# Graph attention kernel, edge loop: three PSUM buffers for the edge products, the softmax in one bank with its key rows read from DRAM, and a later place for sums and exponents

## What is computed

```python
q, k, v = x @ Wq + bq, x @ Wk + bk, x @ Wv + bv      # by head
e  = edge_attr @ We                                  # 106250 x 256 by 256 x 256
kj = k[src] + e
alpha = sum(q[dst] * kj, over the 32 of a head) / sqrt(32)
amax  = segment_max(alpha, dst)
ea    = exp(alpha - amax[dst])
denom = segment_sum(ea, dst)
out   = segment_sum((v[src] + e) * ea / denom[dst], dst) + (x @ Ws + bs)
```

## Time and profile before

| | us |
|---|---|
| median of 3 runs | 2530.81 |
| lowest and highest | 2526.67, 2532.15 |
| the profiled execution, its time | 2519.88 |
| its span in the profile | 2518.1 |
| first and last addition L1059 of the edge loop | 230.1, 1905.4 |
| busy share of the span: PE, DVE, ACT, POOL | 94%, 79%, 62%, 72% |

### The profile page before, as it was taken

The page is one execution under the profiler, slowest core; times in us unless marked ns, Lnnn a source line. Parts: engine busy times, 40 slices in busy tenths (PEclk is TensorE's granted clock), DMA queues, the critical chain, the costliest instruction groups (busy, mean ns, idle before and its releaser), DMA issues. The chain is left out here.

```text
span 2518.1 us, 62222 instructions
## 1 busy us (share of the span) xinstructions
PE 2368.8 (94%) x13314; PEld 1994.0 (79%) x13315; DVE 1990.4 (79%) x5253; ACT 1573.8 (62%) x4349; POOL 1809.0 (72%) x2137
## 2 busy tenths in 40 slices
PE   6998999999999999999999999999995658999998
PEld 2445888888888888888888888888883647999998
DVE  6875999999999999999999999999997872222222
ACT  1122677777777777777777777777774125666665
POOL 4223788888888888888888888888886205666666
PEclk9999999999999999999999999999998558999999
DMA  7325877788788778778877777777772672433443
GB/s 230 129 107 182 243 230 229 227 233 232 225 232 228 222 231 232 230 230 232 233 230 229 232 223 231 233 226 227 232 229 81 193 224 53 71 63 63 69 67 54
DMA packets 337730, 476.37 MB, mean 189 GB/s; under 512 B 61382, under 2 KB 268556, under 8 KB 337116
## 3 DMA queue, kind: packets, MB, share of 16 engines
q0 software_dynamic: 92576, 259.72, 39.2%
q1 hardware_dynamic: 238556, 213.23, 27.7%
q10 hardware_dynamic: 6288, 0.05, 0.2%
HBM read 425.40 MB, written 50.57 MB: 189 GB/s over the span
## 5 line engine op out<-in xcount | busy, mean ns | idle before, releaser
L818 POOL DMA_INDIRECT kv_ring<-vk_table,tab_c x880 | 859.7, 977 | 250.9 <-issue 168.2
L976 PE MATMUL ps_e<-we_sb,aT 128*128 128x256 f32 x3520 | 916.4, 383 | 12.3 <-DVE ve_ke L1065 7.8
L976 PEld LDWEIGHTS ps_e<-we_sb,aT 128*128 128x128 f32 x3520 | 600.6, 191 | 82.7 <-issue 31.3
L1059 DVE TENSOR_TENSOR ve_ke<-kv_ring,ps_e 128x512 f32<-128x512 f32 x880 | 601.4, 683 | 47.9 <-PE ps_e L980 17.9
L828 POOL TENSOR_TENSOR ve_ke<-ve_ke 128x256 f32<-128x256 f32 x880 | 551.2, 630 | 16.9 <-ACT factor L945 3.3
L1029 PE MATMUL ps_u<-ve_ke,sel 128*128 128x264 f32 x1760 | 544.3, 391 | 10.1 <-DVE node_slots L1135 5.6
L980 PE MATMUL ps_e<-q_slots,selT 128*128 x1760 | 517.2, 375 | 0.0
L905 ACT COPY aT<-ps_t 128x256 f32<-128x256 f32 x880 | 325.4, 370 | 283.6 <-PE ps_t L960 246.9
L1135 DVE TENSOR_TENSOR node_slots<-node_slots,ps_u 128x264 f32 x880 | 369.9, 420 | 29.0 <-PE ps_u L1029 25.0
L980 PEld LDWEIGHTS ps_e<-q_slots,selT 128*128 128x128 f32 x1760 | 334.7, 190 | 45.6
L1047 DVE TENSOR_REDUCE alpha<-ve_ke 128x8 f32<-128x256 f32 x880 | 362.9, 412 | 2.0
(11 more groups left out here) (255 smaller groups left out, 2631.3 us busy)
## 6 DMA issues: line engine op xcount, KB each, us to landing
a_ring<-in_edge_attr SPq DMA_DIRECT2D x880, 128.0 KB
loc_c<-loc_table SPq DMA_DIRECT2D x220, 128.0 KB, 3.9
kv_ring<-vk_table,tab_c POOLq DMA_INDIRECT x880
vk_table<-kv_out SPq DMA_DIRECT2D x49, 256.0 KB, 2.0
skip_table<-skip_out SPq DMA_DIRECT2D x49, 128.0 KB, 1.7
skip<-skip_table SPq DMA_DIRECT2D x7, 896.0 KB, 9.5
xn_table<-node_slots SPq DMA_DIRECT2D x7, 896.0 KB, 5.1
w_sb<-in_L_ffn_W SPq DMA_DIRECT2D x2, 2048.0 KB, 10.1
```

The lines of the kernel that those rows point to most:

```text
L818: g.indirect_dma_start(out=kv_ring[:, i % N_KV, :], out_offset=None, in_=vk_table, in_offset=bass.IndirectOffsetOnAxis(ap=tab_c[:, c % N_T ...
L976: t.matmul(ps_e[i % 2][:, 0:D], aT[i % 2][:, k * P:(k + 1) * P], we_sb[:, k, :], start=(k == 0), stop=(k == KD - 1))
L1059: v.tensor_tensor(ve_ke[:, to:ke + 1:ke - to, 0:D], kv.rearrange("p (t d) -> p t d", t=2), e[:, None, :].to_broadcast([P, 2, D]), ALU.add) ...
```

## The change

- ps_e has three buffers (N_E = 3). `project` and the semaphores' first credit follow: item i waits for item i - 3.
- The softmax uses one bank, ps_s. Turned scores and turned shifted scores have the same columns (ps_x = ps_a), so `scores` now waits for the exponents of the chunk before, and `turn_scores` waits for the shift before its first product.
- TensorE's `keys` is gone. The key rows are written once to two DRAM tables during the projection, and SyncE loads them for each chunk, spread over all partitions, into key_c: two DMAs of 64 KB and 68 KB behind those of run_c and resets. ScalarE's `apart` reads key_c in SBUF, and its copy to key_prev is gone.
- In `minima` the transpose of min_l to 128 columns becomes a product of 8 columns.
- LAG: sum and addition 14 for 13, sel 12 for 11, weighing 15 as before.
- TensorE's parts stand in slots 4, 7 and 12 for 3, 6 and 10; ScalarE's exponents in slot 13 for 11. On VectorE the scans and `own` stay in 3, 4 and 6, the two halves of `least` stand in 7 and 8, the shift in 9. The DMAs of run_c and resets wait for the shift, as before.

The diff, cut to its core (left out: the allocation of tables, the semaphores of the tables' writes and their waits):

```diff
@@ -130,11 +133,14 @@
         run_c = [sb(f"run_c{i}", [P, P], F32, c_soft) for i in range(2)]
+        KW = 2 * P + H
+        key_c = [sb(f"key_c{i}", [P, KW], F32, c_soft) for i in range(2)]
...
         reset_loaded = [sem(f"reset_loaded{i}", c_soft) for i in range(2)]
+        key_loaded = [sem(f"key_loaded{i}", c_soft) for i in range(2)]
@@ -250,7 +260,15 @@
             RUNS_OUT, LOCS_OUT, TAB_OUT = 4, 9, MASKS + 4
+            TABLE_WRITES = 2 + 5 * (2 if n_last else 1)
...
+
+            def load_keys(sp, c):
+                keys = key_c[c % 2]
+                sp.dma_start(keys[:, 0:P], first_table[c * CH:(c + 1) * CH, :].rearrange("(o i) h -> o (i h)", o=1).to_broadcast([P, P])
+                             ).then_inc(key_loaded[c % 2], 16)
+                sp.dma_start(keys[:, P:KW], last_table[c * CH:(c + 1) * CH + 1, :].rearrange("(o i) h -> o (i h)", o=1).to_broadcast([P, P + H])
+                             ).then_inc(key_loaded[c % 2], 16)
@@ -286,6 +304,14 @@
+                def keys_to_tables():
+                    sp.wait_ge(keys_ready, 3)
+                    sp.dma_start(last_table[0:1, :], no_key[:, :]).then_inc(tables_written, 16)
+                    for k, table in enumerate((first_table[0:IT, :], last_table[1:IT + 1, :])):
+                        sp.dma_start(table[0:nf * P, :].rearrange("(b p) h -> p b h", p=P), keys_io[:, k, 0:nf, :]).then_inc(tables_written, 16)
+                        if n_last:
+                            sp.dma_start(table[nf * P:IT, :], keys_io[0:n_last, k, nf, :]).then_inc(tables_written, 16)
@@ -519,7 +548,12 @@
                         v.tensor_scalar(run_f, run_g[:, :, :], BIG, None, ALU.mult).then_inc(tables_ready, 1)
+                        v.memset(no_key[:, :], -BIG).then_inc(keys_ready, 1)
+                        then(v.tensor_scalar(head_row[:, :], iota_free[:, 0:H], BIG / H, None, ALU.mult))
                     else:
+                        for k, e in enumerate((0, P - 1)):
+                            v.tensor_tensor(keys_io[:, k, :, :], run_f[:, :, e:e + 1].to_broadcast([P, IB, H]),
+                                            head_row[:, None, :].to_broadcast([P, IB, H]), ALU.add).then_inc(keys_ready, 1)
@@ -705,18 +737,17 @@
             ps_t = [ps3(f"ps_t3{i}", [P, 512]) for i in range(2)]
-            ps_e = [ps3(f"ps_e{i}", [P, 512]) for i in range(2)]
+            ps_e = [ps3(f"ps_e{i}", [P, 512]) for i in range(N_E)]
             ps_u = [ps3(f"ps_u{i}", [P, 512]) for i in range(2)]
-            ps_ak = ps3("ps_ak", [P, 512])
-            ps_rx = ps3("ps_rx", [P, 512])
-            ps_a, ps_k = ps_ak[:, 0:P], ps_ak[:, P:P + KW]
-            ps_r, ps_x, ps_d = ps_rx[:, 0:KW], ps_rx[:, KW:KW + P], ps_rx[:, KW + P:KW + P + H]
...
-
-            s, at, grant = counters(c3, a_turned=N_A, aT_ready=2, e_ready=2, ve_added=N_KV, kq_ready=2,
+            ps_s = ps3("ps_s", [P, 512])
+            ps_a, ps_r, ps_d = ps_s[:, 0:P], ps_s[:, P:P + KW], ps_s[:, P + KW:P + KW + H]
+            ps_x = ps_a
...
+
+            s, at, grant = counters(c3, a_turned=N_A, aT_ready=2, e_ready=2, ve_added=N_KV, kq_ready=N_E,
...
-                                    am_ready=0, run_by_head=0, keyed=0, keys_apart=0, key_kept=0, offs_ready=0,
+                                    am_ready=0, run_by_head=0, keys_apart=0, offs_ready=0,
@@ -730,9 +761,9 @@
             LAG = dict(weigh=FIRST_WEIGH + N_KV,
-                       select=FIRST_WEIGH,
-                       sum=FIRST_WEIGH + 2,
-                       add=FIRST_WEIGH + 2)
+                       select=FIRST_WEIGH + 1,
+                       sum=FIRST_WEIGH + 3,
+                       add=FIRST_WEIGH + 3)
@@ -795,6 +826,9 @@
                                          ).then_inc(reset_loaded[par], 16)
+                            if c >= 2:
+                                sp.wait_ge(s["keys_apart"], at("keys_apart", c - 2))
+                            load_keys(sp, c)
@@ -919,13 +953,13 @@
                             act.sem_inc(s["act_pace"], 1)
-                            act.wait_ge(s["keyed"], at("keyed", c - 1))
+                            act.wait_ge(key_loaded[1 - par], 32 * ((c - 1) // 2 + 1))
...
                             act.sem_inc(s["act_pace"], 1)
-                            nc.scalar.activation(not_f[:, :], ps_k, ACT.Abs, scale=-1.0, bias=run[:, 0:1])
-                            nc.scalar.activation(not_l[:, :], ps_k, ACT.Abs, scale=-1.0, bias=run[:, P - 1:P]).then_inc(s["keys_apart"], 1)
-                            nc.scalar.copy(key_prev[:, :], run[:, P - 1:P]).then_inc(s["key_kept"], 1)
+                            nc.scalar.activation(not_f[:, :], key_c[1 - par][:, :], ACT.Abs, scale=-1.0, bias=run[:, 0:1])
+                            nc.scalar.activation(not_l[:, :], key_c[1 - par][:, :], ACT.Abs, scale=-1.0, bias=run[:, P - 1:P]
+                                                 ).then_inc(s["keys_apart"], 1)
@@ -945,7 +979,7 @@
-                over_chunks(act, emit, what="select", parts={3: "apart", 4: "offs", 11: "exp"})
+                over_chunks(act, emit, what="select", parts={3: "apart", 4: "offs", 13: "exp"})
@@ -970,14 +1004,14 @@
-                    pe.wait_ge(s["ve_added"], at("ve_added", c * CH + (i - 2)))
-                    pe.wait_ge(s["kq_ready"], at("kq_ready", c * CH + (i - 2)))
+                    pe.wait_ge(s["ve_added"], at("ve_added", c * CH + (i - N_E)))
+                    pe.wait_ge(s["kq_ready"], at("kq_ready", c * CH + (i - N_E)))
                     for k in range(KD):
-                        t.matmul(ps_e[i % 2][:, 0:D], aT[i % 2][:, k * P:(k + 1) * P], we_sb[:, k, :], start=(k == 0), stop=(k == KD - 1))
+                        t.matmul(ps_e[(c * CH + i) % N_E][:, 0:D], aT[i % 2][:, k * P:(k + 1) * P], we_sb[:, k, :], start=(k == 0), stop=(k == KD - 1))
...
                     for part in range(2):
-                        last = t.matmul(ps_e[i % 2][:, D:2 * D], selT[i // SEL % 2][:, i % SEL * P:(i % SEL + 1) * P],
+                        last = t.matmul(ps_e[(c * CH + i) % N_E][:, D:2 * D], selT[i // SEL % 2][:, i % SEL * P:(i % SEL + 1) * P],
@@ -996,30 +1030,21 @@
                                 next_tiles[:] = node_tiles_of(c + 1)
-                        elif kind == "keys":
-                            run = run_c[1 - par]
-                            pe.wait_ge(s["run_by_head"], at("run_by_head", c - 1))
-                            pe.wait_ge(s["shifted_ready"], at("shifted_ready", c - 2))
-                            pe.wait_ge(s["key_kept"], at("key_kept", c - 2))
-                            t.transpose(ps_k[:, KW - P:KW], key_prev[:, 0:1].to_broadcast([P, P]), ident[:, :])
-                            t.transpose(ps_k[:, 0:P], run[:, 0:1].to_broadcast([P, P]), ident[:, :])
-                            t.transpose(ps_k[:, P:2 * P], run[:, P - 1:P].to_broadcast([P, P]), ident[:, :]).then_inc(s["keyed"], 1)
...
                             pe.wait_ge(s["am_ready"], at("am_ready", c - 1))
-                            pe.wait_ge(s["keys_apart"], at("keys_apart", c - 1))
+                            pe.wait_ge(s["ea_ready"], at("ea_ready", c - 2))
...
                             pe.wait_ge(s["scanned"], at("scanned", c - 1))
-                            pe.wait_ge(s["ea_ready"], at("ea_ready", c - 2))
-                            t.transpose(ps_r[:, KW - P:KW], min_l[par][:, 0:1].to_broadcast([P, P]), ident[:, :])
                             t.transpose(ps_r[:, 0:P], scan_b[:, 0:1].to_broadcast([P, P]), ident[:, :])
-                            t.transpose(ps_r[:, P:2 * P], scan_f[:, P - 1:P].to_broadcast([P, P]), ident[:, :]).then_inc(s["min_spread"], 1)
+                            t.matmul(ps_r[:, P:P + H], min_l[par][:, 0:1].to_broadcast([P, P]), ident[:, P - H:P], start=True, stop=True)
+                            t.transpose(ps_r[:, P + H:KW], scan_f[:, P - 1:P].to_broadcast([P, P]), ident[:, :]).then_inc(s["min_spread"], 1)
...
                             pe.wait_ge(s["owned"], at("owned", c - 1))
+                            pe.wait_ge(s["shifted_ready"], at("shifted_ready", c - 1))
...
                             t.matmul(ps_d, min_l[par][:, 0:1].to_broadcast([P, P]), nident[:, P - H:P], start=False, stop=True)
-                            pe.wait_ge(s["shifted_ready"], at("shifted_ready", c - 1))
@@ -1029,7 +1054,7 @@
-                over_chunks(pe, emit, what="sum", parts={0: "keys", 3: "scores", 6: "minima", 10: "turn_scores"})
+                over_chunks(pe, emit, what="sum", parts={4: "scores", 7: "minima", 12: "turn_scores"})
@@ -1048,7 +1072,8 @@
                 def score(c, par, i, meanwhile):
-                    e = ps_e[i % 2][:, 0:D]
+                    ps = ps_e[(c * CH + i) % N_E]
+                    e = ps[:, 0:D]
@@ -1079,6 +1104,7 @@
                     elif part == "own":
+                        dve.wait_ge(s["keys_apart"], at("keys_apart", c - 1))
@@ -1087,19 +1113,19 @@
```

(7 more changed lines are left out.)

21 lines of the change are left out of this document (14 added, 7 removed).

## The result

The changed kernel takes 2541.62 us (median of 15 runs, 2534.93 to 2548.25), the kernel before 2527.2 beside it (15 runs): ratio 1.005, 95% interval 1.0043 to 1.0057. It is slower by 0.5%; the forecast was 2511 and faster.

A forecast was written before the change was run, and what follows sets the result against it. Three nearly full engines (TensorE, VectorE, GpSimd) and their handing over bound the kernel. A chunk of 29.55 + 0.2 + 0.05 = 29.8 saves 25 us in 54 chunks, less 4 and 1: 20, so 2511 us, range 2488 to 2534.

The forecast's parts named there:

- The floor: Edge loop chunk from TensorE's 29.20 + 0.33 waiting or VectorE's 29.25 + 0.3: about 29.55 us, before gathers and restarts.
- cap by ps_u: Two sum buffers limit how far VectorE's addition trails TensorE's product, at most 2.63 us; TensorE waits 0.33 a chunk there.
- key loads at 0: Two more key loads in SyncE's queue ahead of item 0's edge rows: cost 0, from -0.1 to +0.1 a chunk.
- error at the root: The prediction called itself wrong at the root if TensorE waited for edge rows or the 1.765 us item pitch moved.
- exponents and gathers: Gathers queued behind GpSimd's first weighing start later as exponents move: +0.2 us a chunk, from 0 to +1.
- D12: Start of item 12's addition on VectorE, where the exponents were expected to end.
- +4 for late gathers: GpSimd sometimes issues a gather 1.7 to 2.7 us late; shorter leads absorb less of it: +4 us in all.
- 1 us of drain: After the edge loop, sums and additions one item later add an item to the drain: at most 1.8, taken as +1.
- Rival D: Slower: the chain exponents, weighing, gather, addition closes on itself from a landing of 4.95 us; 2544 at 5.2; chance 0.15.
- B: Gathers never late, landing within 4.0 us, so a chunk takes 29.55: 2494 us; chance 0.18.
- C: Third buffer's gain returns as waiting at the sums and own; chunk stays at 30.25: 2531 us; chance 0.13.
- A: The prediction's own sum of all terms: 2511 us, between 2500 and 2524; chance 0.54.

The follow-up runs named there:

- before_keys: Kernel before with two further one-row broadcast loads on SyncE per chunk, ahead of item 0's edge rows, into tiles nothing reads: 2529.88 us, ratio 1.0016.
- loads_late: Changed kernel with SyncE's loads of runs, resets and keys issued ahead of item 4's edge rows instead of item 0's: 2544.03 us, ratio 1.0069 against the kernel before.
- keys_on_act: Changed kernel with turning at 11, exponents at 12, and the key loads issued by ScalarE at item 7: 2515.01 us, ratio 0.9965 against the kernel before.
- keys_act_late: As keys_on_act, with SyncE's loads of runs and resets also moved ahead of item 4's edge rows: 2513.88 us, ratio 0.9957 against the kernel before.
- before_lag14: Kernel before with selection, sums and additions one item later (12, 14, 14) and nothing else: 2534.30 us, ratio 1.0032.
- before_exp_late: Kernel before with only the turning of the scores (10 to 12) and the exponents (11 to 13) two items later: 2568.32 us, ratio 1.017.
- all_early: Changed kernel with undivided least at 7, shift at 8, turning at 10, exponents at 11, SyncE's loads at item 4: 2525.74 us, ratio 1.0002 against the kernel before.
- both_moved: Changed kernel with turning at 11, exponents at 12, and SyncE's loads ahead of item 4's edge rows: 2511.90 us, ratio 0.9949 against the kernel before.
- exp_early: Early exponents: changed kernel with turning of the scores at 11 instead of 12 and exponents at 12 instead of 13: 2518.05 us, ratio 0.9967 against the kernel before.

## Why the prediction was wrong

**The floor was right.** TensorE's and VectorE's needs with the cap by ps_u gave 29.55 a chunk; the chunks without a stall take 29.58 in the median, and the wait at the edge product is gone. The key loads at 0 were right within 0 to 5. Item 0's edge rows have 4.3 us from issue to turning (6.3 before), about the 4 of the prediction, but it set beside them no time for this transfer, which takes 4.0: only 0.2 are left from landing to turning, where 2.6 were, and doubling the loads uses that up. (The 4.6 in the expectation of before_keys is 2.6 when counted to item 0's own turning.) TensorE does wait for edge rows, which the prediction called an error at the root; three runs (loads_late, keys_on_act, keys_act_late) took most of those waits away and won nothing clear of noise by it.

**The step that failed is that of exponents and gathers.** Its exponents end at D12: they do, 0.11 after it. Its lead for item 15, 4.8, came out as 4.83. Its landing, 4.5, came out as a median of 4.42. The error is what was done with the two: a median lead was set against a median landing, the difference was called a shortfall of 0.5 at most, and +0.2 a chunk and +4 for late gathers were put down. But landings spread, one in ten over 5.07, one in a hundred over 5.87. And they lengthen where loads of SyncE or ScalarE meet them, as at item 1. At a lead above 6, as items 14, 15 and 0 had, nearly none of that is felt; at 4.7 to 4.9 a seventh to a fifth is, at item 1 half, and with three engines near full nothing makes it up: over the 52 chunks, one is about 1.1 us longer for each us of stall in it (a fitted line). The price came irregularly, not as the regular wait that the prediction looked for: stalls on gathers rose from 11.4 to 44.8 us, and the time beyond the regular chunk from 0.36 to 1.23 a chunk. The term of 0.2 x 54 + 4, 15 us, measured 47. That is the wrong sign. Of it 24 go with one item of exponents; early exponents leave 0.54 a chunk, 10 us above the kernel before, of which 9 are again stalls on gathers (20.7 against 11.4). These last stand mostly at items 13 and 14, whose leads the prediction doesn't treat: it priced the longer lag at 1 us of drain, and by before_lag14 it costs 8 with two buffers.

**Outside the loop** +1 was forecast and 6.9 measured (2.3 ahead, 4.6 behind). The part ahead is 2.0 in before_keys too, which has no tables but two more loads, and 1.1 in before_exp_late, which has neither. The part behind is hardly the change's: in the twenty profiles it lies anywhere from 612.7 (before) to 617.3 (after), and at 613.6 to 615.7 in the kernels before with only the order or the loads of the loop changed.

**Rival D** gave 2544 by gathers, for 2541.6 measured, but on a condition that didn't hold: no landing of 4.95, and the regular chunk never went to 30.5. Its chain was the right one; it closes by the tail of the landings, not by their middle. Its sign, waits for kv_ring above 0.8 a chunk, was met: 44.8 us are 0.83. **B**, no late gathers at all, was furthest off. The fit of the Trainium skill ("DMA: Bandwidth & Descriptors", Anatomy of one DMA) by which it stood gave an estimate of 3.6 from the start of the issue; the measured median is 4.42, so here the measurement decides. **C** is out, since a chunk without a stall takes 29.58 and not 30.25. Its sign came all the same: TensorE's idle time at the sums is 0.95 a chunk, over the 0.7 named. It is 1.1 in chunks with a stall and 0.5 in those without, so it is in good part VectorE's stalls passed on. **A**'s sum of 2511 is what the kernel reaches with the exponents one item earlier and the late loads, 2511.9; that this is the same number is chance, since the terms differ.

**Open** stays how 14 us of all_early come about, the rest of the 6.9 outside the loop, how the price of the six loads divides between edge rows and gathers, and whether the gain of both_moved over early exponents (6, intervals overlapping) is real.

## What to carry to other kernels

When a change moves a producer later in a queue in which loads stand behind it, compare the loads' lead with the tail of their landing time, not with its median: here the first item of delay was free and the second cost 42 us on the kernel before (TensorE's wait for the mask included). Then look at each load by itself: leads and landings both differ by item. A third buffer needed the lag and the parts moved with it; but what feeds another engine's queue, here the exponents ahead of GpSimd's weighing, must not be moved along with the rest. A shorter pattern chunk is no gain while the mean chunk grows: read both.

## What the runs showed of the hardware

**VectorE and GpSimd hold each other up when both inputs of VectorE's instruction are in SBUF.** With early exponents VectorE's small rescaling falls on GpSimd's weighing. From the trace of both_moved:

```profile
892.00 0.44 DVE L1139 TENSOR_TENSOR node_slots<-node_slots,factor 128x256 f32 x1
892.18 0.73 POOL L862 TENSOR_TENSOR ve_ke<-ve_ke 128x256 f32<-128x256 f32 x1
892.36 0.57 DVE L1140 TENSOR_TENSOR node_slots<-node_slots,factor 128x8 f32 x1
893.06 0.98 POOL L852 DMA_INDIRECT kv_ring<-vk_table,tab_c  x1 [0.16 <-issue]
```

L1140 works on 8 columns and takes 0.57, until 892.93, just after the weighing's end at 892.91; the weighing, begun while L1139 ran, takes 0.73 for its usual 0.62. In 7 chunks in which L1140 met no weighing its mean was 0.156. The backward scan, also SBUF only, went from the first of these rows in the kernel before to the second in the changed kernel:

```profile
L1079 DVE TENSOR_TENSOR_SCAN scan_b<-resets,scan_f 128x128 f32<-128x128 f32 x54 | 22.6, 419 | 0.0
L1104 DVE TENSOR_TENSOR_SCAN scan_b<-resets,scan_f 128x128 f32<-128x128 f32 x54 | 37.1, 688 | 0.0
```

Here a weighing beside it is not enough of a reason. The scan meets one in 45 of 54 chunks of the changed kernel, but in the kernel before it meets one nearly always too. There it begins 0.12 ahead of the weighing and keeps its 0.42, while the weighing takes 0.71. In the changed kernel it begins 0.49 ahead, beside the last part of GpSimd's gather instruction. Why that start costs it 0.27 the runs don't show.

The addition, which has an input in PSUM, keeps its time: 0.682 beside a weighing, 0.684 without. The Trainium skill ("SBUF — State Buffer", SBUF: two separate sides) says that a VectorE instruction with two SBUF inputs and a GpSimd one take the same port pair, whole and in turns; the rows of L1140 and its weighing agree. The rescaling accounts for 0.21 of the regular chunk's rise from 29.58 to 29.91 with early exponents: slot 14, with the rescaling, grew from 2.67 to 2.88 in the median. A further 0.15 appeared at item 3, which these rows don't explain.

**A gather's time is its slowest part's.** The example above had fifteen parts landed at 4.54 us and the last at 5.50. Over all gathers of the changed kernel the last part lands 0.15 us behind the fifteenth in the median, among the slowest tenth 0.8. In all kernels the median over all items was 4.2 to 4.5 us and the highest tenth over 5.0 to 5.7. By item it moves with the loads that other queues issue beside it: item 7's gather took 5.35 where ScalarE issues the key loads there (keys_on_act) and 4.46 where it doesn't (exp_early), item 2's 5.29 in loads_late and 4.66 in the changed kernel.

**SyncE's queue has a limit with a sharp edge.** Two broadcast loads more cost 4 us on the kernel before, where item 0's rows still land 1.3 us before their turning; two more on top of the changed kernel's two cost 38.5, where the 0.2 of that kernel fall to none. A load keeps the queue for 0.43 to 0.59 us, and what waits behind is a ring of four edge-row buffers.
